# Moving the second score pair of a step, the value copies and the projection buffers in a quantised decoder layer

## What is computed

```python
result, ch_bias, n = chunk_decompose(hidden)      # int4 per chunk of 64 rows and channel group
Q = proj(q_weight) * 16 ** -0.5; K = proj(k_weight); V = proj(v_weight)   # proj(w): result @ wq.T + ch_bias @ w.T + b
probs = softmax(einsum('bqhd,bkhd->bhqk', Q, K))  # 32 heads of 16
ctx = einsum('bhqk,bkhd->bqhd', probs, V)         # decomposed once more, then the o projection
x = x + attn(ln(x)); x = x + xattn(ln(x)); x = x + ffn(ln(x))
```

## Time and profile before

| | |
|---|---|
| runs, median (lowest to highest) | 997.08 us (995.59 to 998.17), 3 runs |
| the profiled execution | 992.63 us, span 990.9 us |
| busy: PE, DVE, ACT, POOL | 757.2, 769.6, 628.0, 116.2 us |
| projections with early scores | about 83 to 157 us of the span |
| attention loop | about 157 to 492 us |

### The profile page before, as it was taken

One profiled execution on the slowest core, in us unless ns is written; L12 is line 12 of the kernel. 1 busy time (PEld: TensorE's weight loads), 2 busy tenths in 40 slices (PEclk: granted clock), 3 DMA queues, 4 the chain that ended last, 5 costly groups with the idle time before them and its releaser, 6 DMA issues.

```text
span 990.9 us, 15387 instructions
## 1 busy us (share of the span) xinstructions
PE 757.2 (76%) x5149; PEld 318.5 (32%) x5165; DVE 769.6 (78%) x1055; ACT 628.0 (63%) x1066; POOL 116.2 (12%) x218
## 2 busy tenths in 40 slices
PE   1576988999999999999934824544565559999997
PEld 0432322222222222222311214334334424444443
DVE  7999777999999999999599988688978883632111
ACT  4879435989888888899519217656666746752000
POOL 1200842000000000011000010000002140000001
PEclk9877997999999999999966856567768759999999
DMA  8500864122121212111030001100004830000000
GB/s 297 212 1 1 262 200 129 48 55 56 50 59 49 60 47 58 49 53 33 18 130 0 1 0 43 43 21 22 1 12 176 334 85 1 1 1 2 30 22 32
DMA packets 45733, 66.70 MB, mean 67 GB/s; under 512 B 8940, under 2 KB 23276, under 8 KB 45176
## 3 DMA queue, kind: packets, MB, share of 16 engines
q1 hardware_dynamic: 44408, 61.92, 19.5%
q0 software_dynamic: 1280, 4.20, 1.3%
HBM read 42.50 MB, written 19.14 MB: 62 GB/s over the span
## 4 chain that ended last, share of the span: by engine, by line
PE 50%; DVE 20%; ACT 18%; issue 6%; DMA 3%; POOL 1%; SPq 0%; ACTq 0%; POOLq 0%; DVEq 0%
PE PS L1450 12%; PE PS L1654 8%; PE PS L1665 8%; PE PS L1335 6%; PE PS L1467 6%; ACT slab L1770 4%; ACT slab L1706 2%; PE PS L1364 2%; PE PS L1582 2%; ACT HB L1757 2%; DMA slab<-in_L_ffn_w 2%; DMA slab<-in_x 1%; DVE mx L1039 1%; DVE mx L1038 1%; ACT slab L1677 1%
## 5 line engine op out<-in xcount | busy, mean ns | idle before, releaser
L905 DVE TENSOR_REDUCE SWV<-PS 128x2 f32<-128x1024 f32 x256 | 302.0, 1219 | 16.8 <-PE PS L1335 14.5
L1770 ACT ACTIVATE slab<-PS 128x512 f32<-128x512 f32 x512 | 275.7, 595 | 40.5 <-PE PS L1467 31.5
L1450 PE MATMUL PS<-slab,HB 128*32 128x256 f32 x2048 | 164.3, 393 | 9.9 <-ACT HB L1757 9.6
L1467 PE MATMUL PS<-slab 50*128 50x512 f16 x512 | 125.5, 385 | 3.7 <-ACT slab L1770 1.2
L1335 PE MATMUL PS<-slab 48*128 48x512 f16 x512 | 101.8, 392 | 6.3 <-DVE SWV L905 4.9
L1654 PE MATMUL PS<-slab 128*128 128x512 f16 x384 | 86.2, 388 | 1.7 <-DVE slab L1224 1.4
L1665 PE MATMUL PS<-slab 128*128 128x512 f16 x384 | 83.0, 379 | 0.0
L1450 PEld LDWEIGHTS PS<-slab,HB 128*32 128x32 f32 x2048 | 41.6, 108 | 91.1 <-issue 64.9
L1256 DVE SCALAR_TENSOR_TENSOR WOT<-PS,cmax,WOT 128x512 f32<-128x512 f32 x8 | 6.0, 751 | 69.8 <-PE PS L1665 69.8
L1335 PEld LDWEIGHTS PS<-slab 48*128 48x128 f16 x512 | 24.7, 93 | 104.8 <-issue 95.4
L605 POOL COPY HB<-slab 128x64 f32 (+1 forms) x128 | 24.5, 236 | 285.0 <-PE PS L1450 284.9
(11 more groups left out here) (305 smaller groups left out, 1196.8 us busy)
## 6 DMA issues: line engine op xcount, KB each, us to landing
slab<-in_L_ffn_w SPq DMA_DIRECT2D x2, 4096.0 KB, 14.7
q_split<-slab SPq DMA_DIRECT2D x24, 256.0 KB, 2.7
k_split<-slab SPq DMA_DIRECT2D x24, 256.0 KB, 2.7
slab<-q_split SPq DMA_DIRECT2D x64, 96.0 KB, 2.5
slab<-k_split SPq DMA_DIRECT2D x64, 96.0 KB, 2.5
slab<-in_x SPq DMA_DIRECT2D x4, 1024.0 KB, 12.3
slab<-HB SPq DMA_DIRECT2D x128, 32.0 KB
slab<-in_fside_BxS2xS SPq DMA_DIRECT2D x4, 1024.0 KB, 5.5
```

Source lines behind the costliest of these rows:

```text
L905: nc.vector.tensor_reduce(NM[:, ring].rearrange("p (a x) -> p a x", a=2)[:, :, x], PS[:, bank:bank + 2, :], AX.X, ALU.max, negate=True).th ...
L1450: ins = nc.tensor.matmul(PS[32 * h:32 * h + 32, 6, cols], VST[:, r % 2, k, h, :], PROB[:, k, h, cols], start=k == half == 0, stop=k == KB ...
L1467: nc.tensor.matmul(PS[:, st_bank(2 * s + a), :], KP[rows, r, p, P * k:P * k + P], QP[rows, r, p, :], start=True, stop=True).then_inc(st_re ...
L1770: nc.scalar.activation(PROB[:, k, 2 * a + p], PS[:, st_bank(t), :], ACT.Exp, scale=score_scale).then_inc(probs, 1)
```

## The change

Seven edits:

1. TensorE: `projected(u)` is divided into its two banks, `projected(u, 0)` and `projected(u, 1)`. The second score pair of step u - 1 is moved from the end of step u - 1 to between these two halves of step u.
2. ScalarE: the copies of values 0 and 1 are moved ahead of the first high half.
3. ScalarE: the constant rows are filled slot by slot, four instructions of a quarter of the size, after the high half and value copy of steps 1 to 4. SyncE waits for the slots accordingly.
4. VectorE: the copies into `s0col` are moved ahead of `bias_parts()`, in both quantisations.
5. The three `XF` buffers get other places in the slab.
6. ScalarE: the wait for the last subtraction before the loop becomes three waits, for subtractions 14, 15 and 16, before the second, third and fourth exponential of body 0.
7. VectorE: `weight_maxima(0)` is moved ahead of `second_norm(0)`.

```diff
-        XF = [slab[3][:, 1024 * n:1024 * n + 1024] for n in range(1, 4)]
+        XF = [slab[3][:, 1024 * n:1024 * n + 1024] for n in (3, 1, 2)]
...
-                    sp.wait_ge(kp_ready, 1)
+                    sp.wait_ge(kp_ready, 2)
...
+                    sp.wait_ge(kp_ready, RING)
                     sp.wait_ge(split_out[2], 48)
...
-                bias_parts()
                 for u in range(2):
                     ins = nc.vector.tensor_copy(s0col[64 * u:64 * u + 64, :],
                                                 s0[64 * u:64 * u + 64, :].rearrange("p (t u) -> p u t", u=2)[:, u])
                     own(ins)
+                bias_parts()
...
+            weight_maxima(0)
             second_norm(0)
-            weight_maxima(0)
             prepare(0)
...
-            def projected(u):
+            def projected(u, q):
...
-                for q in range(2):
-                    for i in range(CT):
-                        nc.tensor.matmul(PS[:, qk_banks(u) + q, :], WB[:, m, i, P * o:P * o + P], QT[:, 2 * half + q, i],
-                                         start=i == 0, stop=False)
+                for i in range(CT):
+                    nc.tensor.matmul(PS[:, qk_banks(u) + q, :], WB[:, m, i, P * o:P * o + P], QT[:, 2 * half + q, i],
+                                     start=i == 0, stop=False)
...
             for u in range(2, NT):
-                projected(u)
+                projected(u, 0)
+                for n, (j, x) in early_pairs(u - 1)[1:]:
+                    early_scores(n, j, x)
+                projected(u, 1)
                 projected_bias(u)
-                early = early_pairs(u)
-                for n, (j, x) in early[:1]:
+                for n, (j, x) in early_pairs(u)[:1]:
                     early_scores(n, j, x)
...
                 values(u)
                 values_bias(u)
-                for n, (j, x) in early[1:]:
-                    early_scores(n, j, x)
...
             quantise(1)
-            nc.scalar.activation(KP.rearrange("p r h q -> p (r h q)"), ones[:, 0:1].broadcast_to([P, RING * 2 * S]), ACT.Copy,
-                                 scale=ROW_UNIT).then_inc(kp_ready, 1)
-
+            def value_copy(u):
+                act.wait_ge(v_mm, u + 1)
+                nc.scalar.activation(V[:, u // KB, :, u % KB], PS[:, 6 + u % 2].rearrange("p (g c) -> p g c", g=NG), ACT.Copy,
+                                     scale=s0col[:, u:u + 1]).then_inc(v_scaled, 1)
+            def unit_rows(r):
+                nc.scalar.activation(KP[:, r].rearrange("p h q -> p (h q)"), ones[:, 0:1].broadcast_to([P, 2 * S]), ACT.Copy,
+                                     scale=ROW_UNIT).then_inc(kp_ready, 1)
+            for u in range(2):
+                value_copy(u)
             for u in range(NT):
...
-                act.wait_ge(v_mm, u + 1)
-                nc.scalar.activation(V[:, u // KB, :, u % KB], PS[:, 6 + u % 2].rearrange("p (g c) -> p g c", g=NG), ACT.Copy,
-                                     scale=s0col[:, u:u + 1]).then_inc(v_scaled, 1)
+                if u >= 2:
+                    value_copy(u)
+                if 1 <= u <= RING:
+                    unit_rows(u - 1)
...
-            act.wait_ge(qk_l, NT)
-
...
+                    if isinstance(i, int) and i == 0 and 1 <= t <= 3:
+                        act.wait_ge(qk_l, NT - 3 + t)
```

More of the change, by code:

```diff
@@ L1394, in values_bias @@
                                  stop=True).then_inc(v_mm, 1)
-            projected(0)
+            for q in range(2):
+                projected(0, q)
             values(0)
-            projected(1)
+            for q in range(2):
+                projected(1, q)
             projected_bias(0)
```

## The result

| | before | after |
|---|---|---|
| runs, median (lowest to highest) | 997.02 us (992.33 to 998.17), 12 runs | 990.42 us (988.94 to 992.07), 11 runs |
| the profiled execution (span) | 992.63 us (990.9) | 991.71 us (990.0) |
| busy: PE, DVE, ACT, POOL | 757.2, 769.6, 628.0, 116.2 us | 763.0, 768.6, 628.9, 117.9 us |

The ratio is 0.9947, with a 95% interval of 0.9929 to 0.9964: 5.3 us faster (3.6 to 7.1), on a forecast of 3.8 us. One further execution of 3631 us is left out as disturbed. The medians lie further apart, 6.6 us, since the times of before fall into clusters and its median is in one of the upper ones. The median after is just under the lower end of the forecast range (990.8); the ratio on the 997.08 of the forecast gives 991.8. Between the two profiled executions there is only 0.9 us; why that is so belongs to the explanation.

What follows compares the result with a forecast made beforehand. VectorE was taken to bound the attention loop, a closed ring of 5.00 us a step projection steps 9 to 14. The terms 4.06 + 0.55 + 0.9 - 1.7 gave 3.8 us off 997.08: 993.3 us, range 990.8 to 996.8.

Steps and rivals of the forecast that it cites:

- Edit 1, 4.06 us: Projection steps 9 to 15: moving the second score pair between projection halves gains 3.15 plus 0.91 us, bounds 2.8 to 4.8.
- 21.85 us: Second pair of step 9 to that of step 14: 5 x 4.24 + 0.65 us, against 25.0 before.
- the split at 0.11 us: TensorE's projection: two halves of four matmuls take 1.94 us where eight in one take 1.83.
- a plain step: Projection steps 9 to 14: 4.24 us each, from TensorE's work of 4.19 and small waits.
- the 0.5 us charged for line 912: VectorE behind a head group's last maxima: line 912 and its follower, about 0.65 us together, lengthen one step by 0.5.
- Step 15's share: Second pair to end of projection in step 15: 0.32 + 0.97 us instead of 0.39 + 1.83, gaining 0.91.
- Edits 2 and 3, 0.55 us: Start of projections: step 4's scaling 0.55 us earlier, VectorE and GpSimd waiting by turns; bounds 1.7 gain, 1.2 loss.
- Rival E: Before step 6 TensorE idles about 1.3 us, the clock falls for 10 us, costing 5.1: 998.4 us; chance 0.08.
- A clock of 0.50 between 100 and 150 us: Sign of a wrong prediction: the clock at 0.50 anywhere from 100 to 150 us in the next profile.
- Edits 5 and 6, 0.9 us: Entry of the attention loop: the first exponential needs no subtraction and starts 0.9 us earlier, taken in full; bounds 0 to 0.9.
- Edit 4: nothing: Both quantisations: column copies ahead of bias parts delay TensorE's first value bias 0.4 us, hidden by other work; no effect.
- Edit 7, a loss of 1.7 us: Start of the second block: VectorE's weight maxima and GpSimd's power run one behind the other, losing 1.7 us; bounds 0.1 to 1.8.

Runs made afterwards that it cites:

- values_only: Kernel before with only the value copies moved ahead, constant rows filled in four parts, column copies ahead of the bias parts: 991.9 us, ratio 0.9964.
- the second profile: Kernel before, unchanged, run and profiled once more: 997.35 us median, ratio 1.0008; the profiled execution 998.46 us.
- fill_step6: Changed kernel with edit 7 undone and eight unread matmuls where TensorE waits ahead of step 6: 989.93 us, ratio 0.9936.
- cast_later: Changed kernel with edit 7 undone and the identity cast moved from ahead of step 4's scaling to behind step 7's: 986.7 us, ratio 0.9908.
- buffers_only: Kernel before with only the XF buffers dealt anew and the wait for the last subtraction made into three: 996.8 us, ratio 1.0011.
- warm_entry: Changed kernel with edit 7 undone and six unread matmuls where TensorE waits for the last value copy: 991.17 us, ratio 0.9948.
- maxima_back: Changed kernel with edit 7 undone, weight_maxima(0) behind second_norm(0) again: 989.95 us, ratio 0.9943.
- maxima_reduce: Changed kernel with the first weight's maxima made by one tensor_reduce instead of two tensor_tensor: one run, 992.53 us.

## Why the prediction was right or wrong

**Edit 1, 4.06 us: right, by its own steps.** From the second pair of step 9 to that of step 14 it forecast 21.85 us, and the profile after has 127.40 to 149.25, which is 21.85. TensorE as the new pace and the split at 0.11 us are in the chain. That the sum agrees to the hundredth is luck all the same, since two of its terms were off and cancel: a plain step is 4.29 and not 4.24, 0.25 us over five, and the 0.5 us charged for line 912 are 0.2 (4.51 for that step; TensorE waited 0.15). Step 15's share, 0.91 (its own terms give 0.93), is 0.87. Alone the edit brought 4.1 us.

**Edits 2 and 3, 0.55 us: the local time nearly right, the worth open.** The scaling of step 4 came 0.47 us earlier (109.41 to 108.94), although VectorE itself was 0.95 us late in this execution from the inputs on. The waiting by turns took up most of that lateness: line 852 had to wait for GpSimd anyway. Where VectorE was on time, it came 0.78 earlier behind the end of ScalarE's quantisation (`values_only`). What the step left out is the wait of TensorE in step 2 for a value copy that stood behind 3.60 us of constant rows. I saw TensorE idle only from VectorE's side, as something that costs nothing since VectorE sets the time of step 4. In the one profile I had, that was so: the clock was at its lower level at 94 to 97 us, where nobody waited, TensorE came late to the wait and left it at 2.4 GHz. In the second profile TensorE comes early, idles 3.29 us, and the 1.2 GHz fall on step 3; the last scaling is 2.8 us later behind the first. `values_only` has no such wait, and brought 3.6 us in the total and not 0.55, of which its profile shows 1.8 at most. The profile I predicted from (992.63) was of a rarer kind, and I noted that it lay 4.45 us under the median without asking why.

**Rival E came true in small.** TensorE idled 1.80 us ahead of step 6 (I had 1.3) and the clock fell: from the scaling of step 4 to that of step 9 it took 14.50 us before and 15.99 after, 1.5 us lost. I gave it 0.08 with a stretch of 10 us; the stretch was 3.4. A clock of 0.50 between 100 and 150 us was also among the prediction's own signs of being wrong, and it is there, at 109.9 to 113.3. `fill_step6` and `cast_later` say that the idle time is the cause at this place; at step 2, `buffers_only` idled 3.18 us and kept its clock. The Trainium skill, "TensorE: Matmul & The Clock Gate", section "What's actually happening", has it as a rule that throttled is the default and activity releases it; at step 6 the traces agree (1.00 with the wait filled; 2.41 to 3.39 us for eight matmuls after a wait of 1.8 us), at the entry of the loop filling one wait did not help.

**Edits 5 and 6, 0.9 us: right for the first exponential, not shown for what follows.** ScalarE's start moved from 2.32 to 1.59 us behind the last value copy, 0.73, and by 0.9 in `buffers_only`. Body 0 kept it in these two profiles (0.9 and 1.7 us at the first context copy), but over all profiles the spread at that place is larger than the term, and `buffers_only` shows nothing in the total.

**Edit 4: nothing,** as said: line 970, right behind VectorE's passes of the second quantisation, starts 3.8 us earlier (549.76 to 545.93 us), which is the lead that the kernel had by then.

**Edit 7, a loss of 1.7 us: the mechanism right, the size wrong.** It measured 0.88. The term that was mis-sized is 1.69 + 1.22 + 0.69 laid end to end: the power was lengthened by 0.90 us only. Two readings fit the rows. Either it waits for the first of the two (line 990 of before) and runs beside the second (991). Or it does some 0.86 us of its work before it needs its inputs, waits for the end of both and then takes the 0.83 us that lie between the end of 991 and its own. No run tells them apart. Line 855 was the wrong row to size it by: there both instructions are long.

**The sum.** Rise of 4.06 + 0.47 + 0.73, less 1.5 for the clock at step 6 and 0.88 for edit 7, is 2.9 us against the first profile; at 590 us of the span the lead is 3.2. Of that, 2.1 were lost between 590 and 763 us, where nothing was changed. From line 985 to the last line 1061 the fourteen profiles take between 186.4 and 190.8 us without any pattern I can name. Against the second profile of before, the changed kernel has its last value copy 6.7 us earlier and ends 6.7 us earlier. So the two profiles of before put the gain at 0.9 and 6.7 us, and the measured 5.3 lies between. That the slow step 3 is what makes it more than 2.9 is argued, not shown. The 86 executions of before that the runs above were compared with fall into three groups: 19 under 994 us, 50 from 995 to 997.6, 17 above. The first and the last group have a profile, the largest has none. Nor do the parts add up to the whole: 4.1 for edit 1 and 3.6 for edits 2 to 4, less 0.9 for edit 7, are 6.8 us, which is more than 5.3 though within the intervals.

## What to carry to other kernels

When the profiled execution is 4 us quicker than the median, take a second profile of the same kernel before costing anything: here it showed a term of 2.8 us that the first one lacked. An idle stretch of TensorE that costs nothing by the waits can cost one to three microseconds by the clock behind it, so look at who is next on TensorE, not only at who waits. Removing the wait (the cast moved: 4.4 us up to the last value copy, 3.3 in the total) was worth more than filling it (1.8 and nothing). And a VectorE instruction of 0.22 us took 2.14 behind a GpSimd subtraction: put such a one where GpSimd is idle.

## What the runs showed of the hardware that was not expected

Two `tensor_tensor` with both inputs in SBUF, 1.22 and 0.69 us, ran at full pace beside the power on GpSimd and lengthened it by 0.9 us only, not by 1.9; with one input in PSUM they didn't lengthen it at all. TensorE idled 3.18 us in one profile and kept 1.00, and in four others idled 1.8 us ahead of step 6 and fell to 0.50. A reduction over 128 x 2048 elements with the four tiles innermost took 3.61 us, while the same size with contiguous rows takes 2.25 to 2.29 (lines 731 and 732 of before). And where VectorE's first scaling lay 1.0 to 1.3 us later against ScalarE's first value copy (`after` and `warm_entry`, against `values_only`, `maxima_back`, `fill_step6` and `maxima_reduce`), the scaling of step 4 came only 0.3 us later: the waits on GpSimd took up the rest.
